# The softmax squares stored and fetched ahead of x in one DMA queue, and the odd-sized buffers moved to the end of memory

## What is computed

```
q = x @ w_q.T ; k = ctx @ w_k.T ; v = ctx @ w_v.T
probs = softmax(q @ k.T / sqrt(512))
x1 = x + alpha * (probs @ v) @ w_o.T

g = g_w @ ctx + g_b ; theta = theta_w @ x1 + theta_b ; phi = phi_w @ ctx + phi_b
W = (theta.T @ phi) / 512 ; y = (W @ g.T).T
out = batch_norm(w_w @ y + w_b) + x1
```

## Time and profile before

| | |
|---|---|
| median of three runs | 440.23 us |
| the profiled execution | 439.35 us |
| its span, first to last instruction | 437.6 us |
| mean granted clock of TensorE | 0.984 |
| TensorE busy (PE) | 400.7 us, 92% |
| weight loads (PEld) | 331.7 us, 76% |
| VectorE (DVE) | 292.0 us, 67% |
| ScalarE (ACT) | 189.5 us, 43% |
| DMA moved | 68.13 MB, mean 156 GB/s |

### The profile page before, as it was taken

One profiled execution on the slowest core, in us unless ns is written; L12 is line 12 of the kernel. 1 busy time (PEld: TensorE's weight loads), 2 busy tenths in 40 slices (PEclk: granted clock), 3 DMA queues, 4 the chain that ended last, 5 costly groups with the idle time before them and its releaser, 6 DMA issues.

```text
span 437.6 us, 5814 instructions
## 1 busy us (share of the span) xinstructions
PE 400.7 (92%) x1967; PEld 331.7 (76%) x1967; DVE 292.0 (67%) x567; ACT 189.5 (43%) x385; POOL 1.8 (0%) x7
## 2 busy tenths in 40 slices
PE   8999989999799988999699997999799996999855
PEld 5888867897578866898488975788678985788643
DVE  5994559764687638865487647876397647876464
ACT  3575435622455314733346224644247224553231
POOL 1000000000000000000000000000000000000000
PEclk9999999999899998999989999999999999999989
DMA  8992643196324854087322863168430963028302
GB/s 262 345 336 97 195 119 121 50 305 169 108 92 170 243 166 140 0 288 216 114 101 60 306 178 107 67 205 248 146 120 34 320 174 95 0 82 229 99 24 96
DMA packets 55803, 68.13 MB, mean 156 GB/s; under 512 B 4592, under 2 KB 46320, under 8 KB 52720
## 3 DMA queue, kind: packets, MB, share of 16 engines
q1 hardware_dynamic: 55792, 67.99, 48.5%
HBM read 49.09 MB, written 18.87 MB: 155 GB/s over the span
## 4 chain that ended last, share of the span: by engine, by line
PE 37%; DMA 28%; DVE 11%; SPq 11%; ACT 6%; issue 5%; DVEq 0%; ACTq 0%
DMA moved<-blocks 14%; DMA gram_moved<-gram_blocks 10%; PE bank L302 9%; SPq L216 9%; PE bank L303 9%; PE bank L304 9%; PE bank L361 5%; PE bank L331 5%; DMA probs<-moved 4%; DVE x_lo L660 2%; DVE xb L812 2%; ACT x_hi L492 2%; DVE c_sides L660 2%; DVE phi_blocks L796 2%; SPq L202 1%
## 5 line engine op out<-in xcount | busy, mean ns | idle before, releaser
L302 PE MATMUL bank<-c_sides,qk_hi 128*128 128x512 f32 x128 | 51.0, 399 | 0.0
L303 PE MATMUL bank<-c_sides,qk_hi 128*128 128x512 f32 x128 | 50.8, 397 | 0.0
L302 PE MATMUL bank<-ov_hi,c_sides 128*128 128x512 f32 x128 | 50.7, 396 | 0.0
L304 PE MATMUL bank<-ov_hi,c_sides 128*128 128x512 f32 x128 | 50.6, 395 | 0.0
L303 PE MATMUL bank<-ov_lo,c_sides 128*128 128x512 f32 x128 | 50.5, 394 | 0.0
L304 PE MATMUL bank<-c_sides,qk_lo 128*128 128x512 f32 x128 | 50.4, 394 | 0.0
L766 DVE TENSOR_TENSOR pT_lo<-probs,pT_hi 128x512 fp32r<-128x512 f32 x16 | 11.1, 692 | 58.0 <-ACT pT_hi L492 58.0
L302 PE MATMUL bank<-vo_hi,pT_hi 128*128 128x512 f32 x64 | 27.7, 433 | 24.0 <-DVE vo_lo L660 11.9
L492 ACT ACTIVATE pT_hi<-probs 128x512 fp32r<-128x512 f32 x16 | 10.1, 631 | 68.1 <-DMA probs<-moved 68.1
L302 PEld LDWEIGHTS bank<-vo_hi,pT_hi 128*128 128x128 f32 x64 | 12.6, 197 | 32.6 <-issue 30.3
L351 PE MATMUL bank<-tT_hi,xT_lo 128*128 128x256 f32 x128 | 36.2, 283 | 0.0
(11 more groups left out here) (129 smaller groups left out, 899.2 us busy)
## 6 DMA issues: line engine op xcount, KB each, us to landing
cT_raw<-ctx_t SPq DMA_DIRECT2D x8, 1024.0 KB, 4.9
xT_raw<-x_t SPq DMA_DIRECT2D x8, 1024.0 KB, 8.3
c_raw<-ctx_n SPq DMA_DIRECT2D x8, 1024.0 KB, 6.0
xb<-x SPq DMA_DIRECT2D x16, 512.0 KB, 5.3
out<-xb SPq DMA_DIRECT2D x15, 512.0 KB, 3.5
gram_moved<-gram_blocks SPq DMA_DIRECT2D x16, 256.0 KB, 5.9
gram_blocks<-gram_moved SPq DMA_DIRECT2D x64, 64.0 KB, 2.0
moved<-blocks SPq DMA_DIRECT2D x16, 256.0 KB, 2.5
```

The source lines that it names most:

```text
L302: pe.matmul(dst, ahi, bhi, start=(k == 0), stop=False)
L303: pe.matmul(dst, ahi, blo, start=False, stop=False)
L304: mm = pe.matmul(dst, alo, bhi, start=False, stop=(k == k_tiles - 1))
```

## The change

In SP's program the stores of the softmax squares of both b come first, then both fetches, and the loads of x behind them. In the last pair TensorE does theta_rows(0) ahead of w_g_phi; ScalarE and VectorE make u ahead of x1_part(1), and theta_part(0) ahead of t1. In the other pairs their order stays. gram_raw, gram and v are allocated last.

```
-        gram_raw = sb("gram_raw", [P, 2, KS, GW])
-        gram = split("gram", [P, 2, KS, GW])
         u = split("u", [P, 2 * KS, CI])
-        v = sb("v", [P, 2])
...
         inv_sum = sb("inv_sum", [P, 2, KL])
+        v = sb("v", [P, 2])
+        gram_raw = sb("gram_raw", [P, 2, KS, GW])
+        gram = split("gram", [P, 2, KS, GW])
...
                     fetch(gram_blocks[:, b], gram_moved[b], gram_loaded[b])
+                for b in range(2):
+                    sp.wait_ge(blocks_made, two[b + 1])
+                    send(moved[b], blocks[:, b], blocks_stored[b])
+                for b in range(2):
+                    sp.wait_ge(blocks_stored[b], turned[16])
+                    fetch(pT_raw[:, b], moved[b], pT_loaded[b])
                 if not (isinstance(p, int) and p == 0):
                     for b in range(2):
                         sp.wait_ge(stored[b], 16 * p)
                         load_x(p, b)
-                for b in range(2):
-                    sp.wait_ge(blocks_made, two[b + 1])
-                    send(moved[b], blocks[:, b], blocks_stored[b])
-                    sp.wait_ge(blocks_stored[b], turned[16])
-                    fetch(pT_raw[:, b], moved[b], pT_loaded[b])
...
                 if last:
+                    pe.wait_ge(x1_lo, four[2])
+                    theta_rows(0)
                     pe.wait_ge(u_lo, p + 1)
                     pe.wait_ge(x1_made, four[4])
                     w_g_phi(0)
                     w_g_phi(1)
-                    pe.wait_ge(x1_lo, four[2])
-                    theta_rows(0)
                     pe.wait_ge(x1_lo, four[4])
                     theta_rows(1)
...
-                for b in range(2):
-                    for lt in range(KL):
-                        x1_part(b, lt)
-                u_part()
+                for lt in range(KL):
+                    x1_part(0, lt)
                 if last:
+                    u_part()
+                for lt in range(KL):
+                    x1_part(1, lt)
+                if last:
+                    theta_part(0)
                     t1_part(0)
                     t1_part(1)
-                    theta_part(0)
                     theta_part(1)
                     return
+                u_part()
...
-                for b in range(2):
-                    x1_rows(b)
-                    for lt in range(KL):
-                        x1_part(b, lt)
-                u_rows()
-                u_part()
+                x1_rows(0)
+                for lt in range(KL):
+                    x1_part(0, lt)
+                x1_rows(1)
+                if last:
+                    u_rows()
+                    u_part()
+                for lt in range(KL):
+                    x1_part(1, lt)
+                if not last:
+                    u_rows()
+                    u_part()
                 if first:
                     dve.wait_ge(wg_bias_made, 1)
                 if last:
+                    theta_part(0)
                     for b in range(2):
                         t1_rows(b)
                     for b in range(2):
                         t1_part(b)
-                    theta_part(0)
                     theta_part(1)
```

## The result

The changed kernel takes 395.73 us in the median of four runs (395.43 to 397.05), against 440.37 us before: a ratio of 0.8995, 95% interval 0.8962 to 0.9028. I had forecast 402 with a range from 397 to 413.

The account below looks back on a forecast made before the run. TensorE stalled each pair for pT_lo, vo_lo and u_lo behind SP's slow first store; 24.8 + 2.9 + 5.1 + 6.8 = 39.6 off the 437.6 span gives 398.0, 400.7 against the median, 402 with 1.3 allowance; range 397 to 413.

Parts of the forecast that it names:

- Rival (c): SP's first store is slow by itself, 5.9 us in the new place too; 1.2 us a pair lost, 410; chance 0.05.
- rival (d): Slower than before: x so late that it costs more than the waits removed, 447 at 14 us; chance 0.01.
- The first store: SP's first store of softmax squares, now ahead of x, was to take 2.6 us, as in the first pair.
- The chain from vo_hi to u_lo: From the start of vo_hi(1,1) on ScalarE to u_lo done, a middle pair was to keep its 11.8 us.
- The slack before u: In a middle pair u_lo was to be done at 273.75, wanted by TensorE at 274.25: only 0.5 us.
- the 1.3 us: Allowance added over all pairs for slack used up in single pairs before u, taking 400.7 to 402.
- rival b: x loads land late, 9 us after issue: 0.9 us a pair lost, 408; at 11 us, 422; chance 0.13.
- The clock: Three falls of TensorE's granted clock behind waits, 1.7 us lost each, counted as gained: 5.1 us.
- Rival (a): The clock falls stay, since the waits did not set them off; all four staying gives 408.7; chance 0.14.
- The last pair: Its last product comes at 425.7 against 432.50, with 2.1 us of wait for u_lo left; gain 6.8 us.
- Edit 3: Moving gram_raw, gram_hi, gram_lo and v behind all other buffers was to have cost and gain zero.
- The bound of 5 us: Left for the buffers' places: 0.005 us for each of 1000 long products, 5 us either way.

Follow-up runs that it names:

- x between: Changed kernel with SP's order both stores, then the x loads, then both fetches; 421.31 us, ratio 0.9531.
- x behind phi: Changed kernel with the x loads moved behind store and fetch of the phi squares; 426.04 us, ratio 0.9656.

## Why the prediction was right or wrong

- **What bounds the kernel** (stalls of delta behind the first store, the store behind x): right. Rival (c), a first store slow by itself, and rival (d) did not come. All waits for pT_lo and vo_lo are gone, and SP's order alone gives 36.1 of the 44.6 us.
- **The first store, 2.6 us**: 2.4. **The second, 3.5**: never waited for. **Fetch to pT_hi, 3.3 us**: 3.7.
- **The chain from vo_hi to u_lo, 11.8 us**: 240.13 to 251.93, 11.8. **The slack before u, 0.5 us**: 0.18 (wanted at 252.11), because TensorE is faster than I had it. It held in all middle pairs, so the 1.3 us I added for slack used up was not needed for that. That both orders with the old places measured 401.4, between 400.7 and 402, is in part luck: four of its six executions were longer by 1 to 2 us at a lower mean clock, and the two others took 400.1 and 400.3.
- **x and phi late** (rival b): did not happen. The margin of x was 2.7 us and not 0.7; the bound I used for its landing was the landing of the store behind it. What I overlooked is that a late x reaches TensorE in theta_rows(0) before it reaches u.
- **The clock, 5.1 us**: borne out, as a sum over this kernel and not as a rule for each wait. There is no fall in the middle in the eight kernels in which TensorE has no wait over 0.3 us there, nor in the one with stores and fetches interleaved, whose waits before the last pair are 1.6 us at most; there are falls in all four experiments with longer waits (places only, last pair only, x between, x behind phi). Not every such wait brings one: five pairs of the kernel with only the last pair changed have them and no fall. Rival (a) is out for the middle pairs. In the last pair a wait of 1.9 us has no fall behind it in the changed kernel, and has one in the kernel with the new places and 128 bytes more (0.5 from 388 to 391 us).
- The rule of the Trainium skill (TensorE: Matmul & The Clock Gate, HAM oscillation — how this bites in real kernels), taken alone, by which waits as short as those of the earlier trace rows should not matter, does not agree with these runs: where the waits went, the falls went, and with x between the clock fell behind a single wait of 1.81 us.
- **The last pair, 6.8 us**: the last product starts 15.1 us after the last of values(1,1) (373.48 to 388.56), as computed (15.1); 1.9 us of wait for u_lo instead of 2.1. As two single edits its parts are 2.3 in the queue's order and 3.3 in the last pair's (404.76 - 401.43); the remaining 1.2 was to be the clock, and was not measured apart.
- **Edit 3, the places in memory: the step that failed.** "Cost and gain zero" was 5.7 us between the medians, 4.5 of it in the pace of the long products. I leaned on the distances in the earlier trace rows; but the one plain step of a long product there, 261.28 to 261.51, is of ov with the context, which ran at the slower pace, and at two decimals 0.227 and 0.233 both read 0.23. There was nothing faster in these rows to compare with. I also asked about alignment to 64 bytes, by which only u moved, and not about the difference of two operands modulo 256, by which qk, ov, theta and the small weights all moved. The bound of 5 us that I left for it was of the right size; but I laid it on 402, where the allowance of 1.3 was already in, so that 397 stood as the lower end, and the kernel with both (400.7 - 5.7) lies below. A gain above mine had 0.03 of the chances.

The sum with what the runs showed: 440.9 - 36.1 (queue) - 3.3 (last pair) - 5.7 (places) = 395.8, measured 395.7. These are differences along one chain of kernels, so that they add up is no test; 440.9 is the kernel before as timed beside the first of them.

## What to carry to other kernels

Where one queue carries everything, put the transfer whose answer a computing engine waits for ahead of those that are merely large, and move both halves of a round trip: a store or a fetch behind the two loads of x cost 3.5 and 4.5 us more here (5.9 against 2.4, 8.2 against 3.7). When a stall goes, look at what the engine behind it does per instruction; 2 to 6 ns of each of 960 products count only from then on, and the same edit tried earlier showed nothing (0.9991). Start addresses of the two operands of a product are worth one try with a pad of 128 bytes.

## What the hardware showed that I had not expected

- A float32 product of 512 columns with qk has a mean of 389 ns and starts 0.227 us after the one before it where both operands start at the same residue modulo 256 bytes (128 and 128, or 0 and 0), and 393 to 396 ns and 0.233 us where they differ by 64 or by 128. 512 is no better as a modulus: in the old order with the pad c_sides and qk differ by 256 modulo 512, and the products are fast. Why is not shown.
- Products of ov,c_sides stay at 390 to 392 ns where those of qk and pT have 389, with all residues alike. And products of vo,pT, whose operands stand at 128 in both orders, have 390 to 393 ns with the old places and 389 with the new ones. With only qk moved, the first product of x and theta_w, neither of them moved against the other, has 396 ns instead of 392. The difference of the two operands alone does not account for these; they are open.
- TensorE's clock fell to 1.2 GHz behind pairs of waits of less than 2 us each (the earlier trace rows with the earlier trace rows), and once behind a single one of 1.81 us; in other pairs with the same waits it did not.
